# The hand-over to the last stage and its last pair: where the first pair is projected, where statistics stand, and how the last pair is added and stored

## The reference, cut to what matters

```python
x = x + L0(_gn(x), ...)      # 3 routed 3x3 convolution steps, 4 experts
x = x + L1(_gn(x), ...)      # involution: each pixel has its own 3x3 kernel

def L1(x, Wr, br, gamma, beta, mean, var, Ws, bs, Wi, bi):
    r = relu(batch_norm(x @ Wr + br))            # 64 -> 16 channels
    w = (r @ Ws + bs).reshape(B, H, W, 16, 9)    # 16 groups, 9 taps
    xi = x @ Wi + bi                             # 64 -> 64 channels
    patches = 3x3 neighbourhoods of padded xi, reshaped to (16, 4, 9)
    return sum(w * patches, axis=-1)             # over the 9 taps
```

## Time and profile before

| | |
|---|---|
| Median of 3 runs | 698.71 us (698.58 to 699.46) |
| The profiled execution's own time | 699.03 us |
| Its span, first to last instruction | 697.2 us |
| Mean granted TensorE clock | 0.974 |
| TensorE busy | 652.6 us (94%) |
| VectorE busy | 549.3 us (79%) |
| ScalarE busy | 289.0 us (41%) |
| GpSimd busy | 173.9 us (25%) |
| Convolution phases 4 and 5 | 335 to 463.5 us |
| Last stage, first expansion to last addition | 471.9 to 684.2 us |
| Stores of the output | 32, 256 KB each |

### The profile page before, as it was taken

One profiled execution on the slowest core, in us unless ns is written; L12 is line 12 of the kernel. 1 busy time (PEld: TensorE's weight loads), 2 busy tenths in 40 slices (PEclk: granted clock), 3 DMA queues, 4 the chain that ended last, 5 costly groups with the idle time before them and its releaser, 6 DMA issues.

```text
span 697.2 us, 14818 instructions
## 1 busy us (share of the span) xinstructions
PE 652.6 (94%) x6176; PEld 271.0 (39%) x6176; DVE 549.3 (79%) x896; ACT 289.0 (41%) x372; POOL 173.9 (25%) x157
## 2 busy tenths in 40 slices
PE   7878999699999999999999999979999999999993
PEld 7433333223333333333333334424444444444441
DVE  5698957968987988995565789956888888888881
ACT  3753713122322422143002410025677777777742
POOL 2100400008202800450051200212343243243241
PEclk9989999899999999999999999997999999999997
DMA  9920000000000000000000000000111211211212
GB/s 333 206 48 1 2 1 1 1 1 1 3 1 1 2 1 1 1 2 1 1 14 2 1 2 1 1 1 1 27 35 32 60 32 32 61 32 31 61 31 61
DMA packets 54478, 19.66 MB, mean 28 GB/s; under 512 B 51122, under 2 KB 51860, under 8 KB 54420
## 3 DMA queue, kind: packets, MB, share of 16 engines
q1 hardware_dynamic: 54132, 18.57, 10.9%
q10 hardware_dynamic: 288, 0.21, 0.1%
HBM read 10.39 MB, written 8.39 MB: 27 GB/s over the span
## 4 chain that ended last, share of the span: by engine, by line
PE 75%; DVE 13%; ACT 2%; issue 1%; POOL 1%; DVEq 0%; POOLq 0%; ACTq 0%
PE conv L635 36%; PE conv L711 11%; PE att L727 11%; PE att L452 5%; PE att L677 4%; DVE comb L1239 3%; DVE xpad L1158 2%; PE att L699 2%; PE conv L601 2%; PE att L689 2%; PE att L510 1%; DVE x L1215 1%; DVE x L1216 1%; DVE x L1223 1%; DVE stats L1253 1%
## 5 line engine op out<-in xcount | busy, mean ns | idle before, releaser
L635 PE MATMUL conv<-xpad,comb 64*64 64x512 f32 x2592 | 289.8, 595 | 2.8 <-DVE x L1223 2.7
L1453 DVE TENSOR_TENSOR x<-conv,x 128x512 f32<-128x512 f32 x288 | 179.3, 684 | 32.9 <-PE conv L711 31.5
L635 PEld LDWEIGHTS conv<-xpad,comb 64*64 64x64 f32 x2592 | 100.7, 134 | 168.4 <-issue 156.7
L1239 DVE SCALAR_TENSOR_TENSOR comb<-experts,wsel,comb 128x576 f32<-128x576 f32 (+1 forms) x138 | 113.7, 892 | 10.6 <-ACT comb L833 10.5
L711 PE MATMUL conv<-rstack,wse 98*128 98x512 f32 x288 | 97.0, 452 | 3.2 <-POOL rstack L1569 2.6
L833 ACT ACTIVATE comb<-experts,wsel 128x576 f32<-128x576 f32 (+2 forms) x52 | 37.2, 770 | 111.5 <-PE conv L635 69.7
L727 PE MATMUL att<-x,cmp 64*32 64x512 f32 x1280 | 79.7, 596 | 0.0
L711 PEld LDWEIGHTS conv<-rstack,wse 98*128 98x128 f32 x288 | 50.8, 194 | 61.5 <-DVE x L1453 44.4
L1158 DVE SCALAR_TENSOR_TENSOR xpad<-att,x 128x1024 f32<-128x1024 f32 x46 | 54.0, 1215 | 20.4 <-PE att L510 20.2
L1576 POOL TENSOR_TENSOR x<-x,xin 128x1024 f32<-128x1024 f32 x16 | 38.4, 2397 | 124.1 <-ACT x L973 124.1
L843 ACT ACTIVATE x<-conv,bias 128x512 f32<-128x512 f32 x40 | 25.2, 682 | 83.6 <-PE conv L635 83.6
(11 more groups left out here) (179 smaller groups left out, 602.9 us busy)
## 6 DMA issues: line engine op xcount, KB each, us to landing
x<-in_x SPq DMA_DIRECT2D x32, 256.0 KB, 5.1
out<-comb SPq DMA_DIRECT2D x32, 256.0 KB, 3.2
experts<-in_We SPq DMA_DIRECT2D x1, 1152.0 KB
wide<-in_c_wide SPq DMA_DIRECT2D x1, 192.0 KB, 5.5
x<-in_c_sum SPq DMA_DIRECT2D x1, 160.0 KB
small<-in_c_small ACTq DMA_DIRECT2D x1, 142.5 KB, 3.5
map_sel<-in_c_map SPq DMA_DIRECT2D x1, 128.0 KB
wr<-in_Wr SPq DMA_DIRECT2D x6, 4.0 KB
```

Of the source, the lines that this page charges most:

```text
L635: last = nc.tensor.matmul(conv[own[to], h, HW * rows:HW * rows + HW], comb[own[rows], q % 2, n, tap(t)], xpad[own[rows], 2 * (q % 2) + n, ...
L1239: v.scalar_tensor_tensor(comb[:, q % 2, n, cols], experts[:, e, cols], wsel[:, p % 2, j + QP * n, e:e + 1], comb[:, q % 2, n, cols], ALU.m ...
L1453: v.tensor_tensor(img(prod[i])[:, rows, :], img(conv[:, unit, :])[:, rows, :], xip[s][:, kh + 16 * h:kh + 16 * h + 16, kw:kw + W], ALU.mul ...
```

## The change

Five things change; nothing is computed differently.

1. Statistics: quads 16 and 17 are done in phase 4 (at j = 2 and 3), quads 18 and 19 in phase 5 at j = 0 and 1, quad 20 at j = 2, quads 21 and 22 at j = 3. Quad 23's two pairs are done by VectorE inside the first pair's products, after taps 1 and 3.
2. The matmul of the group averages for pairs 0 to 7 moves from quad 23's to quad 22's second half, and `group_norm` and the `wse` step to the top of VectorE's last loop iteration, ahead of `final(22, 1)`.
3. `project(0)` and `project_xi(0)` are issued between quad 23's taps, after tap 6 of half 0 and after tap 2 of half 1.
4. TensorE waits after the convolutions only for `final(23, 0)`; the rest of `final_emptied` is waited for ahead of the second expansion.
5. The last pair: VectorE adds the residual, half of the pixels from PSUM directly and half after a ScalarE copy, in place of ScalarE's four copies and GpSimd's addition; the eight transposes signal in two groups of four; ScalarE copies the first half to `pix`, VectorE the second; SP stores each half of the pair's two images as soon as it is there, with four DMAs.

```diff
@@ sync
-            for n in range(2):
-                store_pair(NP - 2 + n, n, 3 * NP + n)
+            store_pair(NP - 2, 0, 3 * NP)
+            for h in range(2):
+                eng.wait_ge(last_emptied[h], 1)
+                for m in range(2):
+                    eng.dma_start(out[2 * (NP - 1) + m, :, :].rearrange("(p t) c -> p t c", t=T)[:, h * T // 2:(h + 1) * T // 2, :],
+                                  pix[1][:, h * T // 2:(h + 1) * T // 2, 64 * m:64 * m + 64]).then_inc(stored[1], 16)
@@ tensor, beside()
-                    elif at == (3, 1, 4):
-                        group_average(4, slice(0, GP), GP, NP + GP + 2 * (QP - 2))
+                    elif at == (2, 1, 4):
+                        group_average(4, slice(0, GP), GP, NP + GP)
+                    elif at == (3, 0, 6):
+                        eng.wait_ge(att_free[1], sum(u == 1 for u, _ in ATT_USES))
+                        project(0, 0, 0, wr[:, :], AR)
+                    elif at == (3, 1, 2):
+                        project_xi(0, 0, 1)
@@ tensor, after the convolutions
-            eng.wait_ge(final_emptied, 2 * 2 * 2 * QP)
+            eng.wait_ge(final_emptied, 2 * 2 * 2 * QP - 2)
...
                 expand(k, s, 0)
+                if first:
+                    eng.wait_ge(final_emptied, 2 * 2 * 2 * QP)
                 expand(k, s, 1)
...
-            project(0, 0, 0, wr[:, :], AR)
-            project_xi(0, 0, 1)
...
-            turn_back(NP - 1, 3 * NP)
+            eng.wait_ge(misc_free, 3 * NP)
+            eng.wait_ge(last_added, 4)
+            last_cols = fin.rearrange("c (p t) -> c t p", t=T)
+            for t in range(T):
+                turned_t = nc.tensor.transpose(att[:, 1, 128 * t:128 * t + 128], last_cols[:, t, :], ident[:, :])
+                if t % (T // 2) == T // 2 - 1:
+                    turned_t.then_inc(last_turned, 1)
@@ scalar
-            empty_sum(NP - 1)
-            empty_pix(NP - 1, 1, 3 * NP)
+            eng.wait_ge(sum_done, len(ROUNDS) * NP)
+            for n in range(2):
+                rows, bank = sum_of(n, 1)
+                nc.scalar.activation(fin[own[n], HW:S], att[rows, 0, bank], ACT.Copy).then_inc(last_copied, 1)
+            eng.wait_ge(last_turned, 1)
+            eng.wait_ge(stored[1], (NP - 2) * 16)
+            nc.scalar.activation(pix[1][:, 0:T // 2, :], att[:, 1, 0:HW].rearrange("p (t c) -> p t c", t=T // 2), ACT.Copy)\
+                .then_inc(last_emptied[0], 1)
@@ vector, top and end of the loop over quads
+                    if q == QUADS - 1:
+                        use = Use("gn", 4)
+                        group_norm(...)
+                        eng.wait_ge(late_lo, 2)
+                        (the wse step, moved here from behind the loop)
...
+                    if p == LAST and j >= 2:
+                        final_stats(QP * LAST + j - 2)
                     if p == PHASES - 1:
-                        final_stats(QP * LAST + j)
-                        if j:
+                        if j < 2:
+                            final_stats(QP * LAST + 2 + j)
+                        elif j == 2:
+                            final_stats(QP * LAST + QP)
+                        else:
+                            final_stats(q - 2)
                             final_stats(q - 1)
                     if q >= QP * LAST:
                         final(q, 0)
@@ vector, last stage
                 for i in range(TAPS):
                     product(k, s, i, first)
+                    if first and i in (1, 3):
+                        channel_stats(slot(QUADS - 1, i // 2))
...
             involve(NP - 1, 1)
+            eng.wait_ge(sum_done, len(ROUNDS) * NP)
+            eng.wait_ge(fin_ready, NP - 1)
+            eng.wait_ge(misc_free, 3 * NP)
+            for n in range(2):
+                rows, bank = sum_of(n, 0)
+                v.tensor_tensor(fin[own[n], 0:HW], att[rows, 0, bank], xin[own[n], NP - 1, 0:HW], ALU.add).then_inc(last_added, 1)
+            for n in range(2):
+                eng.wait_ge(last_copied, n + 1)
+                v.tensor_tensor(fin[own[n], HW:S], fin[own[n], HW:S], xin[own[n], NP - 1, HW:S], ALU.add).then_inc(last_added, 1)
+            eng.wait_ge(last_turned, 2)
+            eng.wait_ge(stored[1], (NP - 2) * 16)
+            v.tensor_copy(pix[1][:, T // 2:T, :], att[:, 1, HW:S].rearrange("p (t c) -> p t c", t=T // 2)).then_inc(last_emptied[1], 1)
@@ gpsimd
-            finish(NP - 1)
```

More of the change, by code:

```diff
@@ L280, in build @@
         stored = [sem("stored0"), sem("stored1")]
+        last_copied = sem("last_copied")
+        last_added = sem("last_added")
+        last_turned = sem("last_turned")
+        last_emptied = [sem("last_emptied0"), sem("last_emptied1")]
         flat = x[:, :, :].rearrange("p a b -> p (a b)")
@@ L391, in _ @@
                     store_pair(2 * i + n, n, 6 * i + 3 * n + 8)
+            store_pair(NP - 2, 0, 3 * NP)
[4 more added lines that the diff above has]
+                                  pix[1][:, h * T // 2:(h + 1) * T // 2, 64 * m:64 * m + 64]).then_inc(stored[1], 16)
             for n in range(2):
[L393 to L395 removed]
+                eng.wait_ge(stored[n], 2 * 16 * (GP + n))
         @block.tensor
@@ L524, in permute, with project, project_xi @@
                 last.then_inc(att_full[use.unit], 1)
+            def project(k, s, m, weights, rows):
+                if not (isinstance(m, int) and m == 0):
+                    eng.wait_ge(misc_free, m)
+                eng.wait_ge(xn_ready, k + 1)
+                for h, cols in halves():
+                    last = nc.tensor.matmul(att[0:rows, 1, cols], weights, xn[s][:, cols], start=True, stop=True)
+                last.then_inc(misc_full, 1)
+            def project_xi(k, s, m):
+                if m:
+                    eng.wait_ge(misc_free, m)
+                eng.wait_ge(xn_ready, k + 1)
+                for n in range(2):
+                    for h, cols in halves():
+                        rows, bank = sum_of(n, h)
+                        for upper in range(2):
+                            last = nc.tensor.matmul(att[rows.start + 32 * upper:rows.start + 32 * upper + 32, 1, bank],
+                                                    wi[own[n], 64 * n + 32 * upper:64 * n + 32 * upper + 32],
+                                                    xn[s][own[n], cols], start=True, stop=True)
+                last.then_inc(misc_full, 1)
             def beside(p, j, h, t):
@@ L1399, in _ @@
                         permuted(1)
+                    if q == QUADS - 1:
+                        use = Use("gn", 4)
+                        group_norm(att[:, use.unit, 0:2 * GP], slice(0, GP), GP, (att_full[use.unit], use.full), (att_free[use.unit], use.freed))
+                        eng.wait_ge(late_lo, 2)
+                        hi_of = wse[:, :, :].rearrange("p a b -> p (a b)")
+                        v.scalar_tensor_tensor(hi_of, hi_of.bitcast(F32), masks[:, 3:4], st_bd.rearrange("p t c -> p (t c)"),
+                                               ALU.mult, ALU.add).then_inc(wse_ready, 1)
                     if q - 1 >= QP * LAST:
@@ L1430, in _ @@
                         final(q, 0)
-            use = Use("gn", 4)
-            group_norm(att[:, use.unit, 0:2 * GP], slice(0, GP), GP, (att_full[use.unit], use.full), (att_free[use.unit], use.freed))
             final(QUADS - 1, 1)
[L1435 to L1439, removed]
+            eng.wait_ge(final_emptied, 2 * 2 * 2 * QP)
             def product(k, s, i, first):
```

## The result

The changed kernel takes 692.48 us (median of 6 runs, 691.72 to 694.5); the kernel before, run beside it, 698.80 (698.05 to 699.46). The ratio is 0.9913, interval 0.9902 to 0.9924: 0.9% or 6.3 us faster. The forecast was 691.2 with a range of 689.2 to 694.0. The profiled execution took 692.22 us, with a span of 690.4 against 697.2: 6.8 us shorter, where the sum had 7.5.

The account below looks back on a forecast made before the run. TensorE, busy 652.6 of 697.2 us, was taken as the bound, so only its waits at the last stage's hand-over and the tail could yield time: -3.4 and -4.1 sum to -7.5, predicting 691.2 us, range 689.2 to 694.0.

Parts of the forecast that it names:

- forecast A: Whole kernel: the main case, all terms as predicted, 691.2 us, own range 690.2 to 692.4; chance 0.60.
- Part 1: End of phase 4: moved statistics delay `final(19, 0)`, so TensorE stalls before quad 20; +1.7 us, bounds 0 to 3.1.
- Part 2: Quad 23's convolution: two projections between taps lengthen TensorE's stream by 2.83 us, without waits; slack over 3.5 us.
- Part 3: First pair of the last stage: VectorE bounds it; ninth product 14.85 us after the last tap, front -3.4 us net.
- Part 4: Tail after the last addition: shared additions, split transposes and four stores win 4.1 us, bounds 3.2 to 4.5.
- Rival E: Before quad 20: the predicted TensorE stall is absent because the map or `modulate` comes earlier; 689.5 us, chance 0.09.
- Rival D: Quad 23's convolution: TensorE waits for `xn` or the `xi` bank, delaying everything behind; priced at 699.2 us, chance 0.03.
- Rival C: Tail: halved stores gain nothing, each extra issue delaying the next; tail wins only 1 to 2.5 us; chance 0.12.
- The clock: Hand-over and first pair: TensorE busy some two thirds with gaps under 1.3 us, so the full clock should hold.
- Rival B: Stall before quad 20 or first pair: TensorE's clock falls, costing 1.5 to 4 us; 692.7 to 695.2, chance 0.16.

Follow-up runs that it names:

- statistics behind `final`: The changed kernel with the statistics of quads 16 and 17 placed after `final(q, 0)` instead of ahead of it; 690.99 us.
- all together: The changed kernel with quads 16 and 17's statistics after `final(q, 0)`, quad 23's first-half statistics taken earlier, and the last additions shared by three engines; 689.11 us.
- `project_xi` behind: The changed kernel with `project_xi(0)` issued after the last convolution instead of between its taps, `project(0)` staying between them; 694.41 us.
- in halves: The changed kernel with the first-half statistics of quad 23's two pairs taken right after `final(23, 0)`, only second halves and aggregates between the products; 692.01 us.
- without them: The changed kernel without quad 23's statistics, two small memsets of the means in their place, so two pairs are normalised wrongly; 690.69 us.

## Why the prediction was right, and where its sizes were off

The mechanism held in every part, and the forecast A was the case that came, though 692.48 us lies just above A's own range of 690.2 to 692.4. By its own terms:

| Term | Forecast | Profile | Difference |
|---|---|---|---|
| Part 1, the stall | +1.70 | +2.02 | 0.32 |
| Part 2, the projections in the stream | +2.83 | +3.16 | 0.33 |
| Part 3, last tap to ninth product | 14.85 | 14.74 | -0.11 |
| Part 4, the tail | -4.1 | -3.99 | 0.11 |
| Start of the late phases, unchanged code | 0 | +0.07 | 0.07 |

The differences sum to the 0.7 us between the forecast span and the measured one. The rest, 0.6 us to the median, lies between the profiled executions (6.8 us apart) and the medians (6.3).

- **Part 1** had the idle right to the tenth (1.78 for 1.70): each piece of the chain was a row of before. It left out the 0.24 us by which TensorE's stream runs slower right after a stop. Rival E, that the stall isn't there, falls.
- **Part 2** was mis-sized by as much. The slack was right: `xn` was ready at 451.9, 4 us before its use, with GpSimd held up by the `wse` multiply as feared (2.70 us instead of 1.67). The rows that I priced the projections from gave 1.97 and 0.86; they cost 1.89 and 1.02 in the chain. The convolution's own 256 matmuls from 437.55 on take 27.95 us in the chain, and the 256 from 435.49 before took 27.70: 0.25 us more. Far from insertions one takes 0.1073 us (15.45 for 144); the pieces behind an insertion take 0.16 us more than that rate gives, whichever of the three it is. Behind the attention map, whose matmuls have the taps' own 64 x 64 tiles, there is no such surplus (8.59 us for 80). So each of these three insertions cost more than its own row; that the change of tile form is the reason is argued from this, no kernel varied it alone. Rival D falls: no wait at either place.
- **Part 3** was right in its bound (VectorE) and its length. That TensorE takes over as the bound once VectorE is 2.2 us lighter was not in it.
- **Part 4** hit by two errors that cancel, which was luck. The additions took 2.85 us, not 2.6, as each took 0.71 where a product takes 0.626 (why stays open: without any wait between them it is the same 0.71), and the first four transposes were seen after 0.72, not 0.6; the first half was in the buffer 4.31 us after the sum, not 3.93. The store then took 4.68 us to the end of the span, not 4.91. Rival C falls.
- **The clock.** In the changed kernel's two profiles it held at the stall and in the first pair, as forecast, and so it did in the four others whose front is the change's. TensorE was busy in 12.43 of the 14.07 us from 469.4 on, 88% and not two thirds (the ends of matmuls are modelled). Rival B was given 0.16, for a cost of 1.5 to 4 us. None of the ten profiles that have the stall shows a fall there; that a fall is possible at each shorter stall was my own conclusion, and the section that I cited does not say it of one this short. Three of the eleven profiles with the new front show a fall in the first pair, all in kernels with an altered front: statistics behind `final` and all together, which lack the stall, and `project_xi` behind, which has a longer wait. Whether the missing stall plays a part or chance does, one profile of each cannot tell. It cost less than I thought: with statistics behind `final` the first pair took 14.80 us, as at full clock, because VectorE is the bound and hides it; where VectorE was lighter it cost 0.76. In the tail, four of the eleven profiles with the new tail (statistics behind `final`, in halves, without them, and `project_xi` behind) show the eight transposes at the low clock, 1.94 us instead of 1.13, and there the end came 9.41 to 9.47 us after the last sum instead of 8.99. Part of the spread between executions is this. The front's 2.83 us, too, hold only against this execution of the kernel before: where the clock fell later in the old hand-over, the distance that was 22.76 us was 21.94.

## What to carry to other kernels

Work pulled forward into "idle" time of an engine is free only if nothing that another engine waits for is queued behind it: read, for each moved call, what stands after it on its engine and when that is needed. A matmul set between taps of another tile form cost here its own time plus about 0.16 us in the taps behind it, and it needs its inputs long before; it pays when what it releases is a chain of several engines. At a kernel's end, count the instructions in a row on the busiest engine: dividing work among engines helps only if it shortens that row.

## What the runs showed of the hardware that I had not expected

- The granted clock can fall in a stretch without a long wait: in the last kernel, 1.06 us of work in two was followed by a fall after two busier ones, while a 1.78 us stop between full stretches was followed by none in ten profiles. The same first pair, behind a convolution with the stall in it, ran at full clock in another kernel. The Trainium skill ("TensorE: Matmul & The Clock Gate", Part 1, What's actually happening) lets activity decide the clock; a fall behind a thin stretch agrees with that, and why it came in one kernel and not in the other no run here shows.
- Stores of 128 KB landed 2.2 us after their issue, those of 256 KB 3.4 us, and their first bytes moved 0.2 us sooner.
- GpSimd's power of eight columns took 2.70 us instead of 1.65, in all eleven profiles with the new front, while VectorE's `wse` multiply read two operands from SBUF. The Trainium skill ("SBUF — State Buffer", Who interferes with whom) has a VectorE instruction with two SBUF inputs contend with a GpSimd one that reads SBUF; the trace agrees.
